# Two more correction passes in the activation quantizer, and its scale path taken from bf16 to f32

## The reference

```
def act_quant(x):
    scale = 127.0 / jnp.clip(jnp.max(jnp.abs(x), axis=-1, keepdims=True), 1e-05)
    return jnp.clip(jnp.round(x * scale), -128, 127) / scale
def weight_quant(w):
    scale = 1.0 / jnp.clip(jnp.mean(jnp.abs(w)), 1e-05)
    return jnp.clip(jnp.round(w * scale), -1, 1) / scale
h = bit_linear(x, w1)            # einsum of act_quant(x) and weight_quant(w1), 1024 -> 4096
h = depthwise_conv1d(h)          # three taps along the tokens, plus a bias
h = jax.nn.silu(h)
return bit_linear(h, w2)         # 4096 -> 1024
```

## Time and profile before

| what | value |
|---|---|
| median of 3 runs | 10301.86 us (10297.96 to 10302.35) |
| profiled execution | 10309.87 us, span of its slowest core 10308.3 us |
| spans of the eight cores | 10253.7 to 10308.3 us |
| TensorE busy, of the span | 3689.6 us, 36% |
| VectorE busy | 3473.6 us, 34% |
| ScalarE busy | 1908.2 us, 19% |
| data moved, mean rate | 407.65 MB, 40 GB/s |

### The profile page before, as it was taken

One profiled execution on the slowest core, in us unless ns is written; L12 is line 12 of the kernel. 1 busy time (PEld: TensorE's weight loads), 2 busy tenths in 40 slices (PEclk: granted clock), 3 DMA queues, 4 the chain that ended last, 5 costly groups with the idle time before them and its releaser, 6 DMA issues.

```text
span 10308.3 us, 72349 instructions; the slowest of 8 cores (10253.7 to 10308.3 us)
## 1 busy us (share of the span) xinstructions
PE 3689.6 (36%) x21474; PEld 2009.6 (19%) x21474; DVE 3473.6 (34%) x6106; ACT 1908.2 (19%) x3771; POOL 0.2 (0%) x4
## 2 busy tenths in 40 slices
PE   3333333400001434443343343333333332444344
PEld 1111111100001222322211111111121111332222
DVE  1111111123337565555311111111111147555654
ACT  1333233100000000000123333333333210000000
POOL 0000000000000000000000000000000000000000
PEclk9555555655555666666665555555555555666666
DMA  1000000032220433443100000000000001444334
GB/s 55 5 5 5 9 5 5 19 101 82 73 70 17 86 67 77 89 84 78 43 2 5 1 5 5 5 0 5 5 1 5 17 2 39 89 84 89 66 79 109
DMA packets 1187067, 407.65 MB, mean 40 GB/s; under 512 B 1129220, under 2 KB 1162120, under 8 KB 1186696
## 3 DMA queue, kind: packets, MB, share of 16 engines
q1 hardware_dynamic: 1186696, 403.04, 17.4%
HBM read 377.82 MB, written 25.17 MB: 39 GB/s over the span
## 4 chain that ended last, share of the span: by engine, by line
PE 30%; DVE 23%; DMA 18%; issue 13%; ACT 11%; DVEq 4%; SPq 1%; ACTq 0%; POOLq 0%
PE ps L43 27%; DVE FQ L43 10%; DMA W1TS<-w1t 7%; DMA WPF<-w 5%; ACT PPBb L43 4%; DVEq L43 3%; DMA W2TS<-w2t 3%; PE pt L43 2%; DVE HQ L43 2%; ACT PPBa L43 2%; DVE LCOL L43 1%; ACT TMPB L43 1%; DVE TMPA L43 1%; PE pss L43 1%; DVE SR L43 1%
## 5 line engine op out<-in xcount | busy, mean ns | idle before, releaser
L43 PE MATMUL ps<-XQT,W1TS 128*128 128x258 bf16 x4096 | 841.4, 379 | 501.3 <-DMA W1TS<-w1t 476.9
L43 PE MATMUL ps<-HQ,W2TS 128*128 128x256 bf16 x4096 | 553.4, 302 | 981.6 <-DVEq L43 880.4
L43 PE MATMUL ps<-VBb,PPAb 128*128 128x129 bf16 x2048 | 482.5, 297 | 1004.4 <-ACT PPBb L43 1004.4
L43 PE MATMUL pt<-CID,TMPB 128*128 128x128 bf16 (+1 forms) x1456 | 193.9, 280 | 1672.7 <-DVEq L43 1293.9
L43 DVE RECIPROCAL LCOL<-ps 128x3 f32<-128x3 f32 (+2 forms) x160 | 28.7, 180 | 1983.7 <-PE ps L43 1968.1
L43 PEld LDWEIGHTS ps<-XQT,W1TS 128*128 128x128 bf16 x4096 | 495.5, 129 | 842.8 <-issue 679.8
L43 PEld LDWEIGHTS ps<-HQ,W2TS 128*128 128x128 bf16 x4096 | 433.6, 108 | 1089.5 <-issue 1001.9
L43 ACT ACTIVATE PPAb<-ps,LCOL 128x384 bf16<-128x384 f32 (+1 forms) x768 | 419.4, 546 | 995.4 <-PE ps L43 994.8
L43 DVE SCALAR_TENSOR_TENSOR FQ<-ps,CONVP,FQ 128x256 f32<-128x256 f32 x1024 | 495.1, 484 | 82.3 <-issue 6.8
L43 PE MATMUL ps<-VBb,PPBb 128*128 128x129 bf16 x2048 | 519.2, 315 | 0.0
L43 ACT ACTIVATE TMPB<-ps 128x256 bf16<-128x256 f32 (+1 forms) x192 | 87.4, 455 | 2324.5 <-PE ps L43 2324.5
(11 more groups left out here) (137 smaller groups left out, 5291.2 us busy)
## 6 DMA issues: line engine op xcount, KB each, us to landing
W1TS<-w1t SPq DMA_DIRECT2D x512, 256.0 KB, 3.2
W2TS<-w2t SPq DMA_DIRECT2D x128, 1024.0 KB, 7.8
WPF<-w SPq DMA_DIRECT2D x128, 512.0 KB, 3.9
WSAa<-wqkv SPq DMA_DIRECT2D x24, 512.0 KB, 3.8
X<-x SPq DMA_DIRECT2D x1, 8192.0 KB
w1t<-WTS SPq DMA_DIRECT2D x32, 256.0 KB, 2.7
w2t<-WTS SPq DMA_DIRECT2D x32, 256.0 KB, 2.9
out<-X SPq DMA_DIRECT2D x1, 8192.0 KB, 22.0
```

The lines of the kernel that those rows point to most:

```text
L43: r = f(*a, **k)
```

## The change

There are two edits to `build_ffn`, and one constant for them.

The first edit is in the scale step. The casts to bf16 ahead of the two transposes are gone (`TMPB` is no longer used there); TensorE transposes the f32 values themselves against an f32 identity `CIDF`, and the results stand in `PSS` (f32) in place of `PT` (bf16). The second of these transposes now has 2 columns as its stationary operand where it had 128. The new constant `cidf` (64 KB) is loaded by one more DMA at the start.

The second edit is in `qz`. Behind the test above 0.5 stands another test above 1.5, and behind the test below -0.5 another below -1.5, each a `scalar_tensor_tensor` over 2048 elements with a `drain` behind it.

```
@@ build_nc
+    din("cidf", [128, 128], F32)
+        g["CIDF"] = E(nc.sbuf_tensor("CIDF", [128, 128], F32))
-        for nm, dst in (("cid", "CID"), ("chalf", "CHALF"), ("conesf", "CONESF"),
+        for nm, dst in (("cid", "CID"), ("cidf", "CIDF"), ("chalf", "CHALF"),
+                        ("conesf", "CONESF"),
@@ amax
                 v.drain()
-                v.tensor_copy(g["TMPB"][:, 0:TCH], FQ[:, 3584:3584 + TCH])
-                v.drain()
@@ trm
-            def trm(te, vv=max(vv, g["ptv"]["v"])):
+            def trm(te, vv=max(vv, g["pssv"]["v"])):
...
-                    te.transpose(PT[:, i * 128:(i + 1) * 128],
-                                 g["TMPB"][:, i * 128:(i + 1) * 128], CID[:])
+                    te.transpose(PSS[:, i * 128:(i + 1) * 128],
+                                 FQ[:, 3584 + i * 128:3584 + (i + 1) * 128],
+                                 g["CIDF"][:])
@@ smax
-                    v.tensor_reduce(F[:, 40 + i:41 + i], PT[:, i * 128:(i + 1) * 128],
+                    v.tensor_reduce(F[:, 40 + i:41 + i], PSS[:, i * 128:(i + 1) * 128],
...
-                v.tensor_copy(g["TMPB"][:, 0:2], F[:, 40:42])
-                v.drain()
@@ trs
-                te.transpose(PT[:, 0:128], g["TMPB"][:, 0:128], CID[:])
+                te.transpose(PSS[0:2, 256:384], g["FSC"][:, 40:42], g["CIDF"][:])
@@ srow
-                v.tensor_copy(g["SR2"][0:2, 128:256], PT[0:2, 0:128])
+                v.tensor_copy(g["SR2"][0:2, 128:256], PSS[0:2, 256:384])
@@ qz
                     v.scalar_tensor_tensor(B, A, 0.5, B, OP.is_gt, OP.add)
                     v.drain()
+                    v.scalar_tensor_tensor(B, A, 1.5, B, OP.is_gt, OP.add)
+                    v.drain()
                     v.tensor_single_scalar(Ho, A, -0.5, OP.is_lt)
+                    v.drain()
+                    v.scalar_tensor_tensor(Ho, A, -1.5, Ho, OP.is_lt, OP.add)
                     v.drain()
                     v.tensor_sub(Ho, B, Ho)
```

More of the change, by code:

```diff
@@ L910, in smax, with trs @@
                 v.drain()
-                v.tensor_copy(g["TMPB"][:, 0:2], F[:, 40:42])
-                v.drain()
             p.op("vector", smax, "sV", waits=[("sT", tv)])
-            g["ptv"]["v"] = p.val("sV")
+            g["pssv"]["v"] = p.val("sV")
             vv2 = p.val("sV")
-            def trs(te, vv2=max(vv2, g["ptv"]["v"])):
+            def trs(te, vv2=max(vv2, g["pssv"]["v"])):
                 te.wait_ge(p.sems["sV"], vv2)
-                te.transpose(PT[:, 0:128], g["TMPB"][:, 0:128], CID[:])
+                te.transpose(PSS[0:2, 256:384], g["FSC"][:, 40:42], g["CIDF"][:])
             p.op("tensor", trs, "sT")
@@ L1137, in _constants @@
     cid = np.eye(128, dtype=ml_dtypes.bfloat16)
+    cidf = np.eye(128, dtype=np.float32)
     cmask = np.zeros((128, 896), dtype=ml_dtypes.bfloat16)
@@ L1145, in _constants @@
     conescol = np.ones((128, 1), dtype=np.float32)
-    return cid, cmask, chalf, conesf, conescol
+    return cid, cidf, cmask, chalf, conesf, conescol
 def kernel(L0_attn_a_inputs, L0_attn_a_W_qkv, L0_attn_a_W_out,
@@ L1157 @@
     nc = _CACHED[key]
-    cid, cmask, chalf, conesf, conescol = _constants()
+    cid, cidf, cmask, chalf, conesf, conescol = _constants()
     f32 = lambda a: np.ascontiguousarray(np.asarray(a, dtype=np.float32))
@@ L1172 @@
         "w2": f32(L0_ffn_w2),
-        "cid": cid, "cmask": cmask, "chalf": chalf, "conesf": conesf,
-        "conescol": conescol,
+        "cid": cid, "cidf": cidf, "cmask": cmask, "chalf": chalf,
+        "conesf": conesf, "conescol": conescol,
     }
```

## The result

The kernel is slower: 10616.16 us against 10299.91 us (medians of 8 runs each), a ratio of 1.0305 with a 95% interval of 1.0294 to 1.0317. The forecast was 10605, with a range of 10570 to 10645. The profiled execution took 10610.51 us, its slowest core 10609.0 us.

A forecast was written before the change was run, and what follows sets the result against it. The prediction took the quantizing step, VectorE working alone, to be on the path in full. Passes 303.4, scale path -1 and constant load +1 gave +303 us: 10605 us on the median, range 10570 to 10645.

The forecast's parts named there:

- What bounds the kernel: Quantizing step of each FFN chunk, 53.8 us with VectorE alone busy: on the path in full, sixteen times.
- its sign of being wrong: TensorE's wait growing by less than 19 us a chunk, or the load waits moving by more than some 25 us.
- The two passes: Added tests above 1.5 and below -1.5 in the quantizing: 2.37 us each, 128 in all, +303.4 us, nothing hiding them.
- Rival 1: Quantizing, pass below -1.5: its bf16 source gives the bf16 rate, 68 us less, 10537 us; chance 6%.
- The scale path: Scale step: casts gone, transposes in f32; between -10 and +8 us over 16 chunks, taken as -1 us.
- the f32 matmul price: Scale step, upper bound: f32 transposes cost like f32 matmuls, +0.81 us for the pair, +0.3 for the single.
- the lower end of the prediction: Scale step: f32 transposes cost the same as before, so the removed casts save 10 us.
- The load of the constant: Start of the kernel: one more transfer ahead of the first wait, +1 us or nothing, taken as +1.
- Rivals 2, 3 and 5: Chunk loads. 2: quicker, 50 us back, 5%; 3: over 303 us back, not slower, 1%; 5: slower, 50 us more, 3%.
- rival 4: Quantizing: the added passes stand where they are covered; chance under 1%, counted with the third rival.

The follow-up runs named there:

- the finer wait: Kernel after, with the first block of W2 matmuls waiting for each of the four quantizer groups by itself: ratio 1.0259, 46 us less than the kernel after.

## Why the prediction was right, point by point

**What bounds the kernel.** Right. The quantizing step was read as a stretch in which one engine works and all wait; every change made to it came back in the time at its full length. TensorE's wait grew by 296 us in its group (1176.8 - 880.4), short of the forecast 303. That group also holds small waits inside the W2 step, which fell from 5.8 to 1.8 us; ahead of the first block alone it grew by 300.4 us, 18.8 a chunk, and in the first chunk from 54.5 to 73.4, by 18.9. By the letter that is under the 19 us that the prediction set as its sign of being wrong, but that bound was its own forecast rounded up (303 / 16 = 18.96), so it left no room. The growth falls short of it by 1%.

**The two passes.** Right, at 2.35 to 2.38 us each: 304.3 us in the kernel with the passes alone, 300.9 in the kernel after. VectorE's busy time is 3759.7 us, where 3760 was forecast. The pass with a bf16 source cost what the subtraction with the same operands costs, 2291 ns against 2292. Rival 1, a bf16 source lifting the halving, is refuted by that row, and the kernel with two bf16 sources refutes it at its widest. The Trainium skill (Vector Engine (DVE) Microarchitecture Reference, Points that are easy to get wrong) says that this instruction has half the throughput when both sources are in SBUF and not bf16. No run here shows a difference between such sources and bf16 ones: 2292 and 2291 ns.

**The scale path.** Between the bounds of -10 and +8 us, at -3.9 us alone and -3.7 in the kernel after, where -1 was taken. The cost of the f32 transposes is 0.29 us for the pair and 0.11 for the single, some third of the f32 matmul price of 0.81 and 0.3. The rows of the kernel after for the f32 transposes and for the f32 matmuls that spread the scale, and that of the kernel before for bf16 transposes (there over all places of the kernel):

```profile
L43 PE MATMUL pss<-CIDF,FQ 128*128 128x128 f32 x32 | 10.6, 434 | 265.9 <-DVEq L43 265.9
L43 PE MATMUL pss<-SR,CONESF 1*128 1x128 f32 x64 | 19.0, 448 | 15.2 <-DVEq L43 15.2
```

```profile
L43 PE MATMUL pt<-CID,TMPB 128*128 128x128 bf16 x1200 | 160.9, 273 | 1583.3 <-DVEq L43 1293.9 <-ACT TMPB L43 155.7 <-DVE TMPB L43 133.7
```

A transpose is one record of 434 ns, and a matmul of the same type two of 448, so the transpose takes about half. The Trainium skill (TensorE: Matmul & The Clock Gate, Terms) has the transpose mode four times faster for FP32. The traces agree with the direction; the factor they show is 2, with an operand of one row in the matmul, so it isn't a clean comparison. And an f32 transpose isn't as cheap as a bf16 one, so the lower end of the prediction, 10 us saved, was too much.

**The load of the constant.** Taken at +1 us, and too small to tell from nothing (ratio 0.9999). The first wait ended at 32.3 us in before and at 32.9 in the kernel after, on the mean of the eight cores, and at 31.9 with the constant alone; before profiled again has 31.5, and the cores of one execution lie some 3 us apart. So whether that wait hangs on the load issued last stays open.

**The loads of the chunks.** Rivals 2, 3 and 5 did not come. The waits were 470 and 108 us where 477 and 97 had been; on the mean of the eight cores, 461 and 101 where 468 and 99 had been. The order of rival 4 shows in the timeline of the group above.

**What the sum missed.** The measured 316 us (303 to 327 by the interval of the ratio) are 13 above the forecast 303. Ten of them have a place: the first pass of the weight preparation, 339.4 us where it was 329.6, which no step of the prediction looked at, because the change doesn't touch it. It was reproduced in all kernels with another quantizer, and its cause is open. But the stages don't add up to 316. The two profiled executions differ by only 301 us (10583.8 - 10283.1): +300.9 in the quantizing, -3.7 in the scale step, +9.8 in that pass, and -6 in the other stages. The profiled execution of before was itself 10 us above the median of its runs. So the terms that the prediction summed measured 297 in these profiles where it had 303, the first weight pass adds 10, and what the medians have beyond the profiles has no place on record.

## What to carry to other kernels

Where the busy time by stretch shows one engine at work and the others and the DMA at zero, count instructions there and multiply: on such a stretch every drain-separated instruction is worth its whole length, and the total busy share of the engine (34% here) says nothing about it. A chain of six instructions was replaced by one that adds and subtracts a large constant, and this was worth 617 us, where the finer wait was worth 46. When work of TensorE is pulled forward in small pieces under another engine's, look at what the next blocks do: here the second block then carried the rise of the clock and took 1.9 us more, but the third had been waiting for its load, and 3.1 of the 4.2 us won were kept.

## What the runs showed of the hardware that was not expected

- A `scalar_tensor_tensor` took 2291 to 2292 ns for 2048 elements with f32 and f32, f32 and bf16, and bf16 and bf16 sources, whereas a `tensor_tensor` with two bf16 sources took 425 ns for 512 and one of f32 would take some 690 by the rate of the earlier trace rows (an estimate, 158 + 512 x 1.04).
- The time of a stage moved by 3% (329 to 339 us) with edits whose instructions first run some 1000 us later, each time in the same direction; and the kernel with 128 memsets on an idle engine measured 0.2% faster (0.9978, 0.997 to 0.9987). Differences of 0.1 to 0.2% between two builds of this kernel are therefore not evidence on a mechanism, unless the stage concerned shows them.
